# Gated linear attention beside an expert layer: the second half of a sequence attends the first by scores instead of a state

## The chip, the cores and the metric

One core of a Trainium2 chip runs the whole program in one launch. The metric is the device time in microseconds (us). The kernel before took 987.14 us in the median of three timed runs (986.79 to 999.11). The engines are PE (matmul), DVE (vector), ACT (scalar, which also applies the activation tables), POOL (GpSimd, which here also writes the scattered rows) and SP (which issues plain DMAs).

## The reference, cut to what matters

Two layers over 16 sequences of 256 tokens and width 128; each layer is x = x + s * silu(ffn(xn)), where xn is the normed x and s an attention of xn. The change is in the first attention, a gated linear attention with 4 heads (keys of 128, values of 32):

```
q = (x @ Wq).reshape(B, T, H, DK)
k = (x @ Wk).reshape(B, T, H, DK)
v = (x @ Wv).reshape(B, T, H, DV)
gk = jax.nn.log_sigmoid(x @ Wgk1 @ Wgk2 + bgk2) / GATE_NORM
...
G = jnp.cumsum(gc, axis=-2)
qg = qc * jnp.exp(G) * scale
k_intra = kc * jnp.exp(-G)
kg = kc * jnp.exp(G[..., -1:, :] - G)
A = jnp.where(jnp.tril(jnp.ones((C, C), bool)), A, 0.0)   # A = qg @ k_intra^T
o = A @ v + qg @ S
S = S * g_last + kg^T @ v
...
o = o * rsqrt(mean(o * o) + EPS) * gnw * silu(x @ Wg)
s = o.reshape(B, T, H * DV) @ Wo
```

The first layer's ffn is a top-2 mixture of 8 experts: each token's row is scattered to a list of its expert, the lists are worked through in groups of 512 rows, and the results scattered back. The second layer (softmax attention and 16 experts) is not touched.

## The kernel before

Each engine has its own program, written out in the order of one function, `walk` (L302), which calls the same step names on all engines. Semaphores (`sig`) link the engines, and a step's position in `walk` and in the step function is its place in the engine's queue.

**The attention of one batch b** (a sequence, `NB` = 16) takes five ticks. At tick t the function `gla(t, part)`, with parts 0, 1 and 2, works on several batches at once. The sequence is cut in two chunks of 128 tokens, u = 0 and 1:

- tick t = b: `gate_out` (PE, L478) and `gate_logs` (ACT, L980: two Abs, one Exp, one Ln), `gate_sigmoids` (DVE, L1498).
- tick b+1: `decays` on DVE (L1508) is the running sum over the tokens, one scan of 128x1040; `decays` on ACT (L996) makes its two exponentials, P and N; `chunk_ends` on POOL (L1911) multiplies four columns of P and N to the decay over the chunk; `queries_keys` (PE, L491) gives four banks, which `scaled` (DVE, L1537) multiplies by P and N.
- tick b+2: `keys_turned` (PE, L512) turns the first chunk's keys, `keys_moved` (ACT, L1015) copies them out; `scores` (PE, L520) multiplies keys and queries inside each chunk, as a 64x128 and a 64x64 block for each head and chunk; `masked` (DVE, L1520) applies the causal mask.
- tick b+3: `key_values` (PE, L532) makes the state of the first chunk, `states` (DVE, L1529) scales it, `outputs` (PE, L542) adds masked scores times values and, for the second chunk, queries times state.
- tick b+4: normalisation (`output_means` PE, `outputs_scale` ACT, `output_gates` POOL, `gated` DVE), `project` (PE, L561) and `attended` (ACT, L1043).

**Where the ticks lie.** Ticks 0 to 6 stand in the scatter stage, in which POOL writes the rows of all tokens to the expert lists. Ticks 7 to 19 stand in the experts loop, g = 0 to 18, where `TICKS` says which tick a round has: (7, 8, 9, 0, 10, 11, 0, 12, 13, 0, 14, 15, 0, 16, 0, 17, 18, 19, 0). A 0 is a round without a tick, called a bare round below. From tick 7 on (`OUTPUTS_EARLY`) some steps stand in another part. A round is, on every engine:

```
turn(0, g + 1)      # PE turns 512 rows of x, ACT: high part, DVE: low part
gla(t, 0)
ffn0(g, 0); ffn0(g, 1)  # PE up products in two halves, ACT tanh, DVE hidden
gla(t, 1)
ffn0(g, 2)          # PE down products of g - 1, DVE bias, POOL stores
gla(t, 2)
```

**Banks.** All products but the outputs and the gate product share a ring of four PSUM banks (`bank`, L393). A product takes the next bank and waits until the reader of its former contents is done. An up half (`expert_up`, L643) takes two banks. So the order in which steps take banks decides for whom PE waits: in a bare round the takes are turn, two for the first half, two for the second half, down, and the last bank of the second half is the one of the turn, freed by DVE's low part (L1589).

**Names in the rows.** L616 turning of x rows, L559 means, L488 gate product, L539 state product, L661 to L663 up products, L675 down products, L517 key turning; on ACT L990 first gate logs, L1093 tanh, L1019 copy of turned keys, L1005 and L1006 decay exponentials, L881 a table load; on DVE L1550 and L1552 scaled queries and keys, L1514 the scan, L1589 the low part, L1608 the bias; on POOL L1877 scatter of rows, L1896 store of y rows, L1916 `chunk_ends`.

## Time and profile before

| | before |
|---|---|
| timed runs, median (lowest, highest) | 987.14 us (986.79, 999.11) |
| the profiled execution's own time | 995.33 us |
| its span, first to last instruction | 993.3 us |
| mean granted TensorE clock | 0.856 of full |
| PE busy | 738.5 us, 74% |
| DVE busy | 646.1 us, 65% |
| ACT busy | 616.1 us, 62% |
| POOL busy | 453.9 us, 46% |

Busy time is a mean over stages that have different limits. The stages are: norm and routing to 44 us, scatter with ticks 0 to 6 to 160.5, experts with ticks 7 to 19 to 380, and the second layer. The chain that ended last is put down to PE for 33%, ACT 19%, DVE 17%, issue 16% and POOL 9% of the span. The granted clock has two levels, 1.00 (2.4 GHz) and 0.50 (1.2 GHz); a value between them is a mean over a stretch in which it changed.

### The profile page before, as it was taken

The page shows a single profiled execution, that of the slowest core. Times are in us where ns is not written, and L with a number is a line of the kernel's source. Part 1 is how long each engine was busy: PE and PEld are TensorE (multiplying, and loading weights), DVE is VectorE, ACT ScalarE, POOL GpSimd, SP SyncE. Part 2 cuts the span into 40 slices and gives each one's busy share as a digit, 9 for nine tenths or more (in the row PEclk, how much of TensorE's full clock was granted, in tenths as well). Part 3 has the DMA queues.
Part 4 walks back from the last instruction along what each step waited for, and adds up shares of the span by engine and source line. Part 5 has one row for each costly group of instructions (what it writes and reads, how often), then busy time and mean ns, then how long its engine had stood idle before and what let it go on. Part 6 is the DMA issues. An engine that isn't in the chain of part 4 may idle for free.

```text
span 993.3 us, 21325 instructions
## 1 busy us (share of the span) xinstructions
PE 738.5 (74%) x8182; PEld 573.3 (58%) x8182; DVE 646.1 (65%) x1190; ACT 616.1 (62%) x1139; POOL 453.9 (46%) x484
## 2 busy tenths in 40 slices
PE   6756776989898992466954788687978888888650
PEld 4535555878887892344642445456756766766540
DVE  5765655766666643777567554575677777687647
ACT  5653455766667462675641434475778878878775
POOL 4485763242443454100004665223566666756632
PEclk8777879999999996678885777698999999999985
DMA  9811222011111113400003321300111111110054
GB/s 310 304 45 47 62 64 58 20 50 31 47 47 39 46 42 108 115 1 2 1 1 119 121 85 60 86 13 23 30 39 41 34 39 39 42 36 26 19 158 118
DMA packets 62357, 63.81 MB, mean 64 GB/s; under 512 B 7378, under 2 KB 52322, under 8 KB 62132
## 3 DMA queue, kind: packets, MB, share of 16 engines
q1 hardware_dynamic: 53300, 44.02, 15.1%
q0 software_dynamic: 8960, 18.43, 5.7%
q8 instruction: 68, 1.11, 0.5%
q14 instruction: 29, 0.24, 0.1%
HBM read 31.88 MB, written 30.55 MB: 63 GB/s over the span
## 4 chain that ended last, share of the span: by engine, by line
PE 33%; ACT 19%; DVE 17%; issue 16%; POOL 9%; DMA 2%; another core or an unknown queue 2%; SPq 0%; ACTq 0%; POOLq 0%; DVEq 0%
POOL xs L1877 6%; ACT arena L1220 4%; PE bank L721 4%; ACT L881 3%; PE bank L786 3%; PE bank L675 3%; PE bank L798 2%; PE bank L528 2%; POOL ys L1896 2%; DVE arena L1644 2%; DVE arena L1737 2%; ACT arena L1121 2%; DVE arena L1624 1%; DVE arena L1642 1%
## 5 line engine op out<-in xcount | busy, mean ns | idle before, releaser
L1896 POOL DMA_INDIRECT ys<-arena x152 | 172.3, 1134 | 178.4 <-ACT arena L1149 56.3
L1877 POOL DMA_INDIRECT xs<-arena x128 | 131.3, 1026 | 77.1 <-issue 33.5
L1220 ACT ACTIVATE arena<-bank 128x512 f32<-128x512 f32 x192 | 99.1, 600 | 83.6 <-PE bank L786 62.1
L1737 DVE TENSOR_REDUCE arena<-bank 128x2 bf16<-128x512 f32 (+1 forms) x192 | 119.0, 682 | 41.9 <-PE bank L759 37.8
L661 PE MATMUL bank<-arena 128*128 128x128 bf16 x608 | 105.9, 220 | 6.4 <-DVE arena L1589 3.3
L662 PE MATMUL bank<-arena 128*128 128x128 bf16 x608 | 105.9, 220 | 0.0
L663 PE MATMUL bank<-arena 128*128 128x128 bf16 x608 | 105.9, 220 | 0.0
L881 ACT ACT_TABLE_LOAD x72 | 92.4, 1283 | 1.3
L1725 DVE SCALAR_TENSOR_TENSOR arena<-arena,bank 128x512 bf16<-128x512 bf16 x64 | 46.0, 746 | 71.2 <-ACT arena L1193 68.0
L721 PE MATMUL bank<-arena 128*128 128x256 f32 x256 | 67.2, 410 | 0.9 <-issue 0.9
L661 PEld LDWEIGHTS bank<-arena 128*128 x608 | 60.2, 99 | 9.6 <-issue 6.5
L662 PEld LDWEIGHTS bank<-arena 128*128 x608 | 59.8, 98 | 0.3
L663 PEld LDWEIGHTS bank<-arena 128*128 x608 | 59.6, 98 | 0.0
L1828 POOL TENSOR_TENSOR arena<-arena 128x4 f32<-128x4 f32 x16 | 16.2, 1010 | 87.9 <-DVE arena L1323 80.7
L721 PEld LDWEIGHTS bank<-arena 128*128 128x128 f32 x256 | 50.7, 208 | 9.3 <-issue 2.6
L691 PE MATMUL bank<-arena 128*128 x320 | 44.1, 296 | 14.5 <-POOL arena L1942 11.7
L1942 POOL TENSOR_TENSOR arena<-arena 128x1024 f32<-128x1024 f32 x19 | 44.7, 2355 | 20.4 <-ACT arena L1130 19.0
L691 PEld LDWEIGHTS bank<-arena 128*128 128x128 f32 x320 | 42.1, 211 | 17.5 <-issue 17.0
L756 PE MATMUL bank<-arena 32*128 32x256 bf16 (+1 forms) x512 | 22.8, 273 | 38.5 <-DVE arena L1725 14.9
L501 PE MATMUL bank<-arena 128*128 128x256 bf16 x128 | 37.9, 296 | 11.8 <-DVE arena L1518 7.5
L1193 ACT ACTIVATE arena<-bank 128x512 bf16<-128x512 f32 x64 | 36.6, 609 | 16.1 <-PE bank L721 15.6
L1937 POOL TENSOR_TENSOR arena<-arena 128x512 f32<-128x512 f32 x40 | 40.6, 1035 | 10.7 <-DVE arena L1644 10.7
(236 smaller groups left out, 2063.9 us busy)
## 6 DMA issues: line engine op xcount, KB each, us to landing
xs<-arena SPq DMA_DIRECT2D x19, 516.0 KB, 7.2
arena<-xs SPq DMA_DIRECT2D x38, 258.0 KB
arena<-ys SPq DMA_DIRECT2D x32, 256.0 KB, 5.1
arena<-in_MF SPq DMA_DIRECT2D x8, 512.0 KB
ys<-arena POOLq DMA_INDIRECT x152
arena<-in_x SPq DMA_DIRECT2D x8, 256.0 KB, 5.7
arena<-in_W SPq DMA_DIRECT2D x8, 256.0 KB
xs<-arena POOLq DMA_INDIRECT x128
```

Source lines behind the costliest of these rows:

```text
L661: mm(o, hi, b[:, 0, c4], stop=False)
L662: mm(o, hi, b[:, 1, c4], start=False, stop=False)
L663: i = mm(o, lo, b[:, 0, c4], start=False)
L691: i = mm(k[:, 128 * j:128 * j + 128], tb[g % 2][:, h0:h0 + 128], D, start=(c == 0), stop=(c == 1))
L721: j = mm(k[:, 256 * z:256 * z + 256], Wqk[:, c:c + 128], xnT[:, 256 * b:256 * b + 256])
L881: eng.preload_act_table_set(name)
L1220: act(PT[kt_][:, i, gs[0]:gs[0] + len(gs), :], bank_of["s2", b, n, i][:, :].rearrange("p (g q) -> p g q", q=w), ACT.Exp, scale=8 ** -0.5). ...
L1725: stt(T, hiT[n % 2], low_of[n // 2], bank_of["qk1", b, n][:, :], ALU.mult, ALU.add).then_inc(m_qk_moved.sem, 1)
L1737: red(negM[b % 2][:, u, 32 * i + gs[0]:32 * i + gs[0] + len(gs)], kv_, op=ALU.max, negate=True).then_inc(m_max.sem, 1)
L1877: eng.indirect_dma_start(xs[l][:, :], bass.IndirectOffsetOnAxis(ap=slot_i[l][:, m:m + 1], axis=0), xrow[:, t, :], None).then_inc(rows_move ...
L1896: eng.indirect_dma_start(ys[l][:, :], bass.IndirectOffsetOnAxis(ap=yid[g % 4][:, j:j + 1], axis=0), y[:, 128 * j:128 * j + 128], None).the ...
L1942: tt(T, T, U, ALU.mult).then_inc(f1_h.sem, 1)
```

## The change

The state is gone. The second chunk attends the first by scores as well: DVE's `keys_shifted` multiplies the first chunk's scaled keys by the decay over the chunk, PE's `scores` makes four more blocks of 128x128 (`cross`) of them and the second chunk's queries, ACT's `crossed` copies the blocks from PSUM, and `outputs` multiplies the values of the first chunk with them. `keys_turned`, `keys_moved`, `key_values`, `states` and POOL's `chunk_ends` go. The blocks inside a chunk are made whole, one of 128x128 for each head and chunk.

From tick 7 on the places change: `scores`, `crossed` and `masked` stand in part 0, ahead of the up products, the gate logs and the gating; the scan (`decays` on DVE) stands at the end of part 2 of the tick before. POOL's store of the second pair of y rows waits for `o_mean` instead of `kv`.

```diff
...
-        bufK, bufKT = [sb(1024) for _ in range(2)], [sb(512) for _ in range(2)]
+        bufK, bufKX, bufX = [sb(1024) for _ in range(2)], [sb(512) for _ in range(2)], [sb(512) for _ in range(2)]
...
-        bufS = [sb(128) for _ in range(2)]
-        ends = [sb(4) for _ in range(4)]
+        ends = [sb(4) for _ in range(2)]
...
-            def keys_turned(b):
-                k4 = bufK[b % 2].rearrange("p (h c) -> p h c", h=4)
-                k = bank(("kt", b), kt_moved.at(b))
-                eng.wait_ge(*qk_mul.at(b))
-                for h in range(4):
-                    i = eng.transpose(k[:, 128 * h:128 * h + 128], k4[:, h, 0:128], ident)
-                i.then_inc(kt.sem, 1)
...
                 for u in range(2):
                     k, n = bank(("att", b, u), att_masked.at(b, u)), slice(128 * u, 128 * u + 128)
-                    early, late = slice(128 * u, 128 * u + 64), slice(128 * u + 64, 128 * u + 128)
+                    if u == 0:
+                        eng.wait_ge(*qk_mul.at(b))
                     for h in range(4):
-                        mm(k[0:64, 128 * h:128 * h + 128], k4[:, h, early], q4[:, h, n])
-                        i = mm(k[64:128, 128 * h + 64:128 * h + 128], k4[:, h, late], q4[:, h, late])
+                        i = mm(k[:, 128 * h:128 * h + 128], k4[:, h, n], q4[:, h, n])
                     i.then_inc(att.sem, 1)
-            def key_values(b):
-                KT, v = bufKT[b % 2], bufV[b % 3]
-                k = bank(("kv", b), state.at(b))
-                eng.wait_ge(*kt_moved.at(b))
-                eng.wait_ge(*v_moved.at(b))
+                k = bank(("cross", b), cross_moved.at(b))
+                eng.wait_ge(*k_shifted.at(b))
                 for h in range(4):
-                    i = mm(k[:, 32 * h:32 * h + 32], KT[:, 128 * h:128 * h + 128], v[:, 32 * h:32 * h + 32])
-                i.then_inc(kv.sem, 1)
+                    i = mm(k[:, 128 * h:128 * h + 128], bufKX[b % 2][:, 128 * h:128 * h + 128], q4[:, h, 128:256])
+                i.then_inc(cross.sem, 1)
...
-                v, S, A4, o = bufV[b % 3], bufS[b % 2], bufAT[b % 2], o_banks[b % 2]
-                q4 = bufQ[b % 3].rearrange("p (h c) -> p h c", h=4)
+                v, A4, o = bufV[b % 3], bufAT[b % 2], o_banks[b % 2]
                 if b > 1:
                     eng.wait_ge(*o_y.at(b - 2))
+                eng.wait_ge(*v_moved.at(b))
                 for u in range(2):
                     eng.wait_ge(*att_masked.at(b, u))
                     for h in range(4):
                         mm(o[32 * h:32 * h + 32, 128 * u:128 * u + 128], v[:, 128 * u + 32 * h:128 * u + 32 * h + 32], A4[:, u, h, :], start=(u == 0), stop=(u == 0))
-                eng.wait_ge(*state.at(b))
+                eng.wait_ge(*cross_moved.at(b))
                 for h in range(4):
-                    i = mm(o[32 * h:32 * h + 32, 128:256], S[:, 32 * h:32 * h + 32], q4[:, h, 128:256], start=False)
+                    i = mm(o[32 * h:32 * h + 32, 128:256], v[:, 32 * h:32 * h + 32], bufX[b % 2][:, 128 * h:128 * h + 128], start=False)
                 i.then_inc(o_mm.sem, 1)
...
                     if at(t):
                         gate_out(t)
-                    if at(t - 3):
-                        key_values(t - 3)
+                    if at(t - 2) and t >= OUTPUTS_EARLY:
+                        scores(t - 2)
                 elif part == 1:
                     if at(t - 3) and t >= OUTPUTS_EARLY:
                         outputs(t - 3)
-                    if at(t - 2):
-                        keys_turned(t - 2)
+                    if at(t - 2) and t < OUTPUTS_EARLY:
                         scores(t - 2)
                     if at(t + 1):
...
-            def keys_moved(b):
-                eng.wait_ge(*kt.at(b))
+            def crossed(b):
+                eng.wait_ge(*cross.at(b))
                 if b >= 2:
-                    eng.wait_ge(*kv.at(b - 2))
-                act(bufKT[b % 2], bank_of["kt", b][:, :], ACT.Copy).then_inc(kt_moved.sem, 1)
+                    eng.wait_ge(*o_mm.at(b - 2))
+                act(bufX[b % 2], bank_of["cross", b][:, :], ACT.Copy).then_inc(cross_moved.sem, 1)
...
                     if at(t - 4):
                         outputs_scale(t - 4)
+                    if at(t - 2) and t >= OUTPUTS_EARLY:
+                        crossed(t - 2)
                     if at(t):
                         gate_logs(t)
                 elif part == 1:
-                    if at(t - 2):
-                        keys_moved(t - 2)
+                    if at(t - 2) and t < OUTPUTS_EARLY:
+                        crossed(t - 2)
                     if at(t - 1):
...
-            def states(b):
-                kv_, S = (a.rearrange("p (h d) -> p h d", h=4) for a in (bank_of["kv", b][:, 0:128], bufS[b % 2]))
-                eng.wait_ge(*kv.at(b))
-                eng.wait_ge(*p_ends.at(b))
-                if b > 1:
-                    eng.wait_ge(*o_mm.at(b - 2))
-                tt(S, kv_, bc(ends[b % 4], 2, [128, 4, 32]), ALU.mult).then_inc(state.sem, 1)
+            def keys_shifted(b):
+                k4, kx = (a.rearrange("p (h c) -> p h c", h=4) for a in (bufK[b % 2], bufKX[b % 2]))
+                P, N = (a.rearrange("p (h u s) -> p h u s", h=4, u=2) for a in (bufP, bufN))
+                tt(ends[b % 2], P[:, :, 0, 128], N[:, :, 1, 64], ALU.mult).then_inc(k_shifted.sem, 1)
+                eng.wait_ge(*k_shifted.at(b, 0))
+                eng.wait_ge(*qk_mul.at(b))
+                if b >= 2:
+                    eng.wait_ge(*cross.at(b - 2))
+                tt(kx, k4[:, :, 0:128], bc(ends[b % 2], 2, [128, 4, 128]), ALU.mult).then_inc(k_shifted.sem, 1)
             def scaled(b):
...
-                    if at(t - 3):
-                        states(t - 3)
+                    if at(t - 2) and t >= OUTPUTS_EARLY:
+                        masked(t - 2)
                     if at(t - 4) and t >= OUTPUTS_EARLY:
                         gated(t - 4)
-                    if at(t - 1) and t >= OUTPUTS_EARLY:
-                        decays(t - 1)
                 elif part == 1:
-                    if at(t - 2):
+                    if at(t - 2) and t < OUTPUTS_EARLY:
                         masked(t - 2)
                     if at(t + 1):
                         gate_low(t + 1)
...
-                elif at(t - 1):
-                    scaled(t - 1)
+                else:
+                    if at(t - 1):
+                        scaled(t - 1)
+                        keys_shifted(t - 1)
+                    if at(t) and t + 1 >= OUTPUTS_EARLY:
+                        decays(t)
...
-                    eng.wait_ge(*(kv.at(t - 3) if 0 < t < 19 else up[0].at(g, 1) if g < 18 else down[0].at(17)))
+                    eng.wait_ge(*(o_mean.at(t - 4) if t else up[0].at(g, 1) if g < 18 else down[0].at(17)))
...
-            def chunk_ends(b):
-                P, N = (a.rearrange("p (h u s) -> p h u s", h=4, u=2) for a in (bufP, bufN))
-                eng.wait_ge(*pn.at(b))
-                if b >= 4:
-                    eng.wait_ge(*state.at(b - 4))
-                tt(ends[b % 4], P[:, :, 0, 128], N[:, :, 1, 64], ALU.mult).then_inc(p_ends.sem, 1)
...
-                if part == 1 and 0 <= t - 1 < NB:
-                    chunk_ends(t - 1)
...
```

**PE, from the turning to the first up product of an attention round.** Before, where `qk_scaled`, `s0_done` and the like are semaphores named after the step that sets them:

```order
L616 MATMUL bank<-arena 128x128 [waits ld_rows0,qk_scaled]
L616 MATMUL bank<-arena 128x128 x3
L627 TENSOR_LOAD arena
L559 MATMUL bank<-arena 128x256 [waits o_squared]
L488 MATMUL bank<-arena 128x256 [waits decay,gate1_lo]
L488 MATMUL bank<-arena 128x256
L488 MATMUL bank<-arena 128x256 [waits decay]
L488 MATMUL bank<-arena 128x256
L539 MATMUL bank<-arena 128x32 [waits v_moved,k_turned_moved,qk_scaled]
L539 MATMUL bank<-arena 128x32 x3
L661 MATMUL bank<-arena 128x128 [waits x_lo0,s0_done,qk_scaled]
```

Of the change, the same place (L600 is the turning, L544 the means, L486 the gate product, L519 the scores, L524 the cross blocks, L645 the first up product):

```order
L600 MATMUL bank<-arena 128x128 [waits ld_rows0,qk_scaled]
L600 MATMUL bank<-arena 128x128 x3
...
L544 MATMUL bank<-arena 128x256 [waits o_squared]
L486 MATMUL bank<-arena 128x256 [waits decay,gate1_lo]
...
L519 MATMUL bank<-arena 128x128 [waits qk_scaled]
L519 MATMUL bank<-arena 128x128 x3
L519 MATMUL bank<-arena 128x128 [waits qk_scaled]
L519 MATMUL bank<-arena 128x128 x3
L524 MATMUL bank<-arena 128x128 [waits k_shifted,s0_done]
L524 MATMUL bank<-arena 128x128 x3
L645 MATMUL bank<-arena 128x128 [waits x_lo0,att_masked]
```

The scores stand ahead of the ups, and the ups wait for the mask's and the low part's banks.

**ACT, from the high part to the tanh of an attention round** behind a bare one. Before:

```order
L1082 ACTIVATE arena<-bank 128x512 [waits up0,turned0]
L881 ACT_TABLE_LOAD
L1039 ACTIVATE arena<-bank,arena 128x256 [waits o_gated,o_mean]
L1041 ACTIVATE arena<-arena 128x256 [waits o_rs]
L990 ACTIVATE arena<-bank 128x4x128 [waits exp_decay,gate2]
...
L881 ACT_TABLE_LOAD
L1093 ACTIVATE arena<-bank 128x512 [waits f0_h,up0] x2
L1019 ACTIVATE arena<-bank 128x512 [waits kv,k_turned]
L1005 ACTIVATE arena<-arena 128x1040 [waits chunk_ends,qk_scaled,decay]
```

Of the change (L1068 high part, L1003 `crossed`, L974 first gate logs, L1079 tanh, L989 first decay exponential):

```order
L1068 ACTIVATE arena<-bank 128x512 [waits up0,turned0]
L865 ACT_TABLE_LOAD
L1023 ACTIVATE arena<-bank,arena 128x256 [waits o_gated,o_mean]
L1025 ACTIVATE arena<-arena 128x256 [waits o_rs]
L1003 ACTIVATE arena<-bank 128x512 [waits o_mm,att_cross]
L974 ACTIVATE arena<-bank 128x4x128 [waits exp_decay,gate2]
...
L865 ACT_TABLE_LOAD
L1079 ACTIVATE arena<-bank 128x512 [waits f0_h,up0] x2
L989 ACTIVATE arena<-arena 128x1040 [waits k_shifted,qk_scaled,decay]
```

The copy moved from behind the tanh to ahead of the gate logs.

**DVE, from the scaled keys of one round to the hidden values of the next.** Before:

```order
L1552 TENSOR_TENSOR arena<-bank,arena 128x512 [waits att,qk]
L1552 TENSOR_TENSOR arena<-bank,arena 128x512 [waits qk]
L1589 SCALAR_TENSOR_TENSOR arena<-bank,arena 128x512 [waits x_hi0]
L1535 TENSOR_TENSOR arena<-bank,arena 128x128 [waits o_mm,chunk_ends,kv]
L1558 TENSOR_TENSOR arena<-bank,arena 128x256 [waits wo_mm,o_gate]
L1514 SCALAR_TENSOR_TENSOR arena<-arena 128x1040 [waits decay]
```

Of the change (L1541 scaled keys, L1519 and L1524 `keys_shifted`, L1500 the scan, L1580 the low part, L1513 `masked`, L1547 `gated`):

```order
L1541 TENSOR_TENSOR arena<-bank,arena 128x512 [waits att,qk]
L1541 TENSOR_TENSOR arena<-bank,arena 128x512 [waits qk]
L1519 TENSOR_TENSOR arena<-arena 128x4
L1524 TENSOR_TENSOR arena<-arena 128x512 [waits att_cross,qk_scaled,k_shifted]
L1500 SCALAR_TENSOR_TENSOR arena<-arena 128x1040 [waits decay]
L1580 SCALAR_TENSOR_TENSOR arena<-bank,arena 128x512 [waits x_hi0]
L1513 COPY_PREDICATED arena<-arena,bank 128x512 [waits o_mm,att]
L1513 COPY_PREDICATED arena<-arena,bank 128x512 [waits att]
L1547 TENSOR_TENSOR arena<-bank,arena 128x256 [waits wo_mm,o_gate]
```

The scan moved ahead of the low part, and two mask steps stand between the low part and the gating.

## Rows read from the trace of the kernel before

**Rows 1.** Busy time by stretch: PE, PEld, DVE, ACT, POOL, clock, DMA share, GB/s

```profile
160.50:380.00 219.50, 197.48 (x2430) 180.78 (x2430) 139.07 (x223) 146.74 (x225) 87.34 (x107) 0.96 0.15 41
```

**Rows 2.** Who PE waited for, 160 to 345 us: total, times, longest

```profile
PE bank L517 <- ACT arena L1093: 16.7, 9, 2.8
```

**Rows 3.** Timeline of PE: start, duration, engine, line, operation, count

```profile
177.35 0.60 PE L616 MATMUL bank<-arena 128*128 128x128 f32 x4
...
192.93 0.60 PE L616 MATMUL bank<-arena 128*128 128x128 f32 x4
...
194.24 0.98 PE L539 MATMUL bank<-arena 128*128 128x32 f32 x8
...
208.51 0.60 PE L616 MATMUL bank<-arena 128*128 128x128 f32 x4
209.24 0.22 PE L661 MATMUL bank<-arena 128*128 128x128 bf16 x1
...
211.98 2.00 PE L675 MATMUL bank<-arena 128*128 128x128 f32 x16
213.82 0.60 PE L616 MATMUL bank<-arena 128*128 128x128 f32 x4
...
332.71 0.60 PE L616 MATMUL bank<-arena 128*128 128x128 f32 x4
```

**Rows 4.** Timeline of ACT in the round of t=9

```profile
194.89 1.06 ACT L990 ACTIVATE arena<-bank 128x512 f32<-128x512 f32 x2
...
199.44 1.09 ACT L1093 ACTIVATE arena<-bank 128x512 f32<-128x512 f32 x2
200.79 0.60 ACT L1019 ACTIVATE arena<-bank 128x512 f32<-128x512 f32 x1 [0.26 <-PE bank L517]
201.28 1.06 ACT L1005 ACTIVATE arena<-arena 128x1040 f32<-128x1040 f32 x1
```

**Rows 5.** Timeline of DVE, end of round t=9, and the scan of t=10

```profile
206.66 1.28 DVE L1550 SCALAR_TENSOR_TENSOR arena<-bank,arena 128x512 f32<-128x512 f32 x2
207.86 1.28 DVE L1552 TENSOR_TENSOR arena<-bank,arena 128x512 f32<-128x512 f32 x2
209.78 0.69 DVE L1589 SCALAR_TENSOR_TENSOR arena<-bank,arena 128x512 bf16<-128x512 f32 x1 [0.64 <-issue]
...
218.48 2.32 DVE L1514 TENSOR_TENSOR_SCAN arena<-arena 128x1040 f32<-128x1040 bf16 x1
```

**Rows 6.** Timeline of ACT in the round of t=10

```profile
221.76 1.09 ACT L1093 ACTIVATE arena<-bank 128x512 f32<-128x512 f32 x2
```

**Rows 7.** Groups by form: count, busy us, mean ns, idle before

```profile
L1702 DVE TENSOR_TENSOR arena<-arena 128x512 f32<-128x512 f32 x8 | 5.5, 692 | 0.3
```

**Rows 8.** Waits of POOL, 50 to 160 us; timeline of PE at 160 us

```profile
POOL arena L1916 <- ACT arena L1006: 12.2, 4, 5.2
...
160.57 0.66 PE L616 MATMUL bank<-arena 128*128 128x128 f32 x2 [4.46 <-DMA arena<-xs]
```

**Rows 9.** Busy time by stretch around idle stretches of PE, columns as in rows 1

```profile
222.40:224.50 2.10, 2.09 (x16) 1.76 (x18) 1.27 (x2) 1.38 (x3) 0.00 (x0) 0.50 0.55 126
...
200.10:202.70 2.60, 2.53 (x36) 2.13 (x36) 2.00 (x3) 2.34 (x4) 0.00 (x0) 1.00 0.46 102
563.30:565.40 2.10, 0.00 (x0) 0.00 (x0) 0.70 (x2) 0.00 (x0) 1.49 (x3) 1.00 0.73 146
565.40:565.90 0.50, 0.44 (x2) 0.20 (x2) 0.50 (x1) 0.00 (x0) 0.50 (x1) 1.00 0.99 386
...
591.50:593.60 2.10, 0.00 (x0) 0.00 (x0) 0.71 (x2) 0.00 (x0) 1.51 (x4) 1.00 0.73 144
593.60:594.30 0.70, 0.67 (x2) 0.29 (x2) 0.70 (x2) 0.00 (x0) 0.70 (x1) 0.50 0.94 381
```

**Rows 10.** Timeline of POOL in the round of t=9

```profile
197.25 1.99 POOL L1896 DMA_INDIRECT ys<-arena  x1 [0.30 <-issue]
```

More of the change, by code:

```diff
@@ L246, in build @@
         gate2, gate2_ln, decay = sig("gate2", 2), sig("gate2_ln", 4), sig("decay", 5)
-        pn, p_ends = sig("exp_decay", 2), sig("chunk_ends")
+        pn, k_shifted = sig("exp_decay", 2), sig("k_shifted", 2)
         xq_hi, xq_lo = sig("chunk_hi"), sig("chunk_lo")
@@ L250, in build @@
         vv, v_moved = sig("v"), sig("v_moved")
-        kt, kt_moved = sig("k_turned"), sig("k_turned_moved")
+        cross, cross_moved = sig("att_cross"), sig("att_cross_moved")
         att, att_masked = sig("att", 2), sig("att_masked", 2)
-        kv, state = sig("kv"), sig("state")
         o_mm, o_sq, o_mean, o_rs, o_gate, o_y = sig("o_mm"), sig("o_squared"), sig("o_mean"), sig("o_rs", 2), sig("o_gate"), sig("o_gated")
@@ L1001, in decays @@
                     eng.wait_ge(*qk_mul.at(b - 1))
-                    eng.wait_ge(*p_ends.at(b - 1))
+                    eng.wait_ge(*k_shifted.at(b - 1, 0))
                 else:
```

## The prediction, made before the change was run

> **What bounds the kernel now.** I read the page's slices first, then the busy time by stage, then whom PE waits for in the stage in which the change lives, then the timelines of one round there, engine by engine. In the experts-and-attention stage (160.5 to 380 us) PE is busy for 197.5 of 219.5 us, DVE for 139 and ACT for 147 [rows 1]: none is full on its own, so a round is as long as its chain of waits. PE's main wait there is the one before the key turning (L517), for ACT's tanh (L1093): 9 times, 16.7 us, the longest 2.8 [rows 2].
>
> I count a round from the start of the turning of its x rows on PE (L616, time T) to the next. The round of t=9 runs from 192.93 to 208.51, 15.58 us, and the bare round behind it to 213.82, 5.31 us. From 177.35 to 332.71, 155.36 us, lie eight attention rounds, t=8 to 15, and four bare ones of about 5.3 (21.3), so the eight take 134.1 [rows 3].
>
> An attention round has two segments. **T to tanh**: turning, means and gate product keep PE until T+1.31 (194.24) [rows 3]; ACT starts the gate logs at T+1.96 (194.89) and the tanh pair at T+6.51 (199.44) [rows 4]. **Tanh to the next T**, 9.07 us: ACT copies the turned keys behind the tanh pair (200.79) and starts the decay exponentials at tanh+1.84 (201.28) [rows 4]; the gate product's copy, the chunk's low part and the gate sums follow, then DVE writes the scaled queries (206.66 to 207.94) and keys (207.86 to 209.14) [rows 5]. The next turning needs the bank of the second query product, free at 207.94; PE, busy since the end of its wait, comes there at 208.51.
>
> **The change, part by part.** *PE work.* An f32 product 128x128x128 is two passes; the 16 passes of L675 from 211.98 to the turning at 213.82 make 0.115 us a pass [rows 3]. Per batch 4 turnings, 16 half-block products in pairs and 4 state products go; 8 whole blocks and 4 cross blocks come, 24 passes, 2.76 us. By the counts PE loses some 0.5 us a batch, which alone shortens no round in which PE waits.
>
> *ACT: `crossed` stands ahead of the gate logs.* Its copy waits for the last cross block. PE can begin the scores at T+1.31 and needs 2.76, so the block is there at about T+4.1. The copy holds ACT for 0.49 (200.79 to 201.28) [rows 4]; the logs start at T+4.6 instead of T+1.96, the tanh at T+9.2 instead of T+6.51: +2.7. *ACT: `keys_moved` is gone from behind the tanh.* The exponentials start at tanh+1.13 instead of +1.84, and all down to the scaled queries moves up by 0.71: the bank is free at tanh+7.8 and the next T is at tanh+7.85 instead of +9.07, PE no longer being the later one, since its scores are done: -1.2. Together a round is 9.2+7.85 = 17.05 us. Behind a bare round (t=10, 12, 14) ACT also loads a table first, and its tanh is at T+7.94 now (221.76 from 213.82) [rows 3, 6]; that load ends before the cross block does, so these rounds become 17.05 as well. Eight rounds: 136.4 against 134.1, **+2.3**; so little because the three reload rounds, the longest now, get shorter and the five others longer.
>
> *DVE: the scan stands ahead of the x low part.* The keys are scaled by 209.14, tanh+9.70, and 0.71 sooner is tanh+8.99 = T+1.14. Then come `keys_shifted`, a 128x4 product (0.2, an estimate: nearest is the 128x512 one, of which it is a small part) and a 128x512 product from SBUF (0.69) [rows 7], and the scan (2.32), all before L1589 (0.69), whose end frees the turn bank [rows 5]: about T+4.95, against T+1.96 now (210.47). In a bare round the ring of four banks gives that bank to the second half of the up products. Both halves take 2.74 now (209.24 to 211.98) and the down products 1.84 [rows 3], so the next T is at 4.97+1.37+1.84 = 8.2 against 5.3. A scan stands in front of four bare rounds: 4 x 2.9 = **+11.5**. In attention rounds the ups wait for that bank too, and for `masked` (T+5.7), but they end by T+8.5, before ACT is ready for the tanh at T+9.2: nothing; that ACT wait is the cover, and without it each would cost up to 2.
>
> *Round t=7* starts its logs as late, +2.7, and gains the 0.7: **+2.0**. *Rounds t=16 to 19* have no logs, so the 0.5 us of PE work shows in each, and t=16 stalls less: **-3**, an estimate with bounds 0 and -5.
>
> *Scatter stage, t=1 to 6.* `chunk_ends` goes from POOL, where scatter descriptors stand behind it; it held them for 12.2 us in four waits on ACT's exponentials. Behind the last scatter PE waits 4.46 us for the rows, until 160.57 [rows 8]: at most that is to be had. Against it, `crossed` stands ahead of the exponentials there, where PE runs at half clock in part, and I count some 3 us of new ACT wait over t=3 and t=6. **-1**, bounds -4 and +4.
>
> *POOL's store* waits for `o_mean` instead of `kv`, which comes sooner in a round: nothing, stores wait for no one else here.
>
> *Clock.* In a bare round PE would be idle from about T+2.55 to T+4.95, 2.4 us. After an idle of 2.1 the clock was still 1.00 once (565.4) and 0.50 once (593.6), after 2.8 it was 0.50 (222.4), after 1.4 it was 1.00 (200.1) [rows 9]. If it falls, 5.5 us of work behind the idle do what 2.75 would: 4 x 2.75 = 11. The rows split, so I take half, **+5.5**. [...]
>
> Sum: 2.3+11.5+2.0-3-1+5.5 = **+17.3**. The profiled execution took 995.3 (span 993.3); the median of the timed runs is 987.1, 8.2 below it and inside their spread (986.8 to 999.1). The sum is a difference of rounds and is set on the median: **1004.5 us**.
>
> **The rivals.** *More clock lost (0.14).* In t=10, 12 and 14 PE has its outputs done at T+7.8 and the tanh at T+9.8: 2.0 idle, between the 1.4 that held and the 2.1 that went both ways. If it falls there, three rounds pay 1.5 to 3 each and all bare rounds pay: 987+12+11+4.5 to 9 = 1015 to 1019. Against: the 2.8 stalls of just these rounds, with their low clock, go.
>
> *The scan stays off the path (0.13).* If the second ups of a bare round had their bank as early as now, 11.5 and 5.5 would fall away: 988, no change. For it: DVE is busy only 63% of the stage [rows 1]. Against: the low part is behind the scan in program order, and the ring has no other bank.
>
> *POOL late (0.06).* The scan now lies where POOL writes the first two y rows of a round. A y row written beside the scan took 1.99 us [rows 10]. The Trainium skill (GPSIMD Engine Reference, Specifications) says that DVE and GpSimd contend for SBUF when DVE reads two SBUF inputs; the 1.99 agrees. Were two rows late by 1 us in eight rounds and waited for, 1004.5 would become 1012 to 1020. Against: no wait of DVE for y stores shows before the stage's end.
>
> *It gets faster (0.05).* One mechanism: the cross block is there when ACT arrives. Then `crossed` costs 0.5, the tanh is at T+7.0 and a round 14.9, eight 119, -15; with the -3 and -4 of the last rounds and the scatter stage and the scan hidden, 967. It turns on the block's end: at T+2.0 it would hold, at T+4.1 it doesn't, and PE cannot begin before T+1.31 [rows 3].
>
> **How the numbers follow.** The forecast (0.62) has its own range, 994 (clock held, scatter stage -4) to 1013 (clock lost in all bare rounds, scatter stage +2). The range of 8 in 10, 991 to 1018, leaves out the fast case (0.05), most of the no-change case (0.08) and the far ends of the slow rivals (0.07). Under 2% (19.7 us, 1006.9) a measurement of this kernel can hardly tell a change from none. Of the forecast 0.22 lies above that, with 0.14 and 0.06 of the two slow rivals: slower 0.42; faster 0.04; within 2% 0.54.
>
> **What would show it.** In the profile after: gate logs 4.6 us behind T (1.96 now), ACT waiting for the cross block ahead of its copy; attention rounds of 17.0, all alike; bare rounds of 8 us, PE waiting 2.4 us for the low part; no tanh wait before scores; PE at 0.50 or at 1.00 behind the bare rounds' idle, which settles the clock term; less than 4.46 us of waiting for rows at the stage's start. I am wrong if attention rounds stay at 15.6 or less, if bare rounds stay at 5.3, or if the scatter stage moves by over 4 us.

## The result and the profile after

The changed kernel takes 1000.85 us in the median of 18 runs (992.10 to 1004.39), the kernel before, beside it, 988.46 (984.21 to 999.11). The ratio is 1.0119, with a 95% interval of 1.0099 to 1.0140: about 12 us slower, inside the 2% that was named as no change. The profiled execution took 999.84 us, its span is 998.0, and the mean granted clock 0.867 (0.856 before).

The page's busy times of the changed kernel, over the whole span:

```profile
PE 729.2 (73%) x7862; PEld 565.5 (57%) x7862; DVE 650.7 (65%) x1206; ACT 612.6 (61%) x1139; POOL 457.1 (46%) x468
```

PE has 9 us less to do and the kernel takes longer: busy time decides nothing here, as [rows 1] said. Whom the engines wait for, 150 to 345 us, in the changed kernel (total, times, longest; L645 is the first up product, L473 stands behind the outputs, L499 is the query and key product, L1079 the tanh, L1003 the copy of the cross blocks, L524 their product):

```profile
PE bank L645 <- DVE arena L1580: 13.1, 8, 2.2
PE bank L473 <- ACT arena L1079: 12.3, 8, 2.3
PE bank L499 <- DVE arena L1504: 4.9, 7, 2.2
PE bank L600 <- DMA arena<-xs: 2.1, 2, 1.6
...
ACT arena L1079 <- PE bank L647: 19.1, 8, 4.2
ACT arena L1003 <- PE bank L524: 16.2, 9, 3.4
```

The one wait of [rows 2], 16.7 us for the tanh ahead of the key turning, has become three: for DVE's low part (L1580) ahead of the ups, for the tanh (L473), and for the chunk's low part (L499). ACT has a new one, 16.2 us in nine rounds, for the cross blocks.

The round of t=9 of the changed kernel, which begins at 189.27 and answers to [rows 3 to 6] (timeline; L600 turning, L974 first gate logs, L989 first exponential, L1541 scaled keys, L1524 `keys_shifted`, L1500 the scan, L1580 low part), and the bare round behind it:

```profile
189.27 0.66 PE L600 MATMUL bank<-arena 128*128 128x128 f32 x4
...
192.43 1.06 PE L524 MATMUL bank<-arena 128*128 128x128 f32 x8
...
193.52 0.60 ACT L1003 ACTIVATE arena<-bank 128x512 f32<-128x512 f32 x1 [2.14 <-PE bank L524]
...
194.01 1.08 ACT L974 ACTIVATE arena<-bank 128x512 f32<-128x512 f32 x2
...
194.76 0.22 PE L645 MATMUL bank<-arena 128*128 128x128 bf16 x1 [1.28 <-DVE arena L1580]
...
198.59 1.09 ACT L1079 ACTIVATE arena<-bank 128x512 f32<-128x512 f32 x2
...
199.24 0.67 PE L473 MATMUL bank<-arena 128*80 128x128 f32 x4 [0.84 <-ACT arena L1079]
...
199.56 1.07 ACT L989 ACTIVATE arena<-arena 128x1040 f32<-128x1040 f32 x1
...
204.72 1.28 DVE L1539 SCALAR_TENSOR_TENSOR arena<-bank,arena 128x512 f32<-128x512 f32 x2
...
206.06 0.65 PE L600 MATMUL bank<-arena 128*128 128x128 f32 x4
...
207.30 0.69 DVE L1524 TENSOR_TENSOR arena<-arena 128x512 f32<-128x512 f32 x1
...
207.91 2.32 DVE L1500 TENSOR_TENSOR_SCAN arena<-arena 128x1040 f32<-128x1040 bf16 x1
...
210.15 0.67 DVE L1580 SCALAR_TENSOR_TENSOR arena<-bank,arena 128x512 bf16<-128x512 f32 x1
...
210.96 0.22 PE L645 MATMUL bank<-arena 128*128 128x128 bf16 x1 [2.16 <-DVE arena L1580]
...
214.14 0.60 PE L600 MATMUL bank<-arena 128*128 128x128 f32 x4
```

The round takes 16.79 us (15.58 before): the copy at T+4.25 has waited 2.14 for the cross blocks, the logs are at T+4.74, the tanh at T+9.32, the next turning at tanh+7.47. The bare round takes 8.08 (5.31 before): DVE has `keys_shifted` and the scan in front of the low part, and PE stands for 2.16 us.

All rounds from the first turning on, each the distance between two turnings in the timeline of PE (us). In t=7 the first turning is that of the very first rows. In brackets, where a bare round follows:

| round | before | before, run again | changed |
|---|---|---|---|
| first turning at | 160.6 | 154.9 | 150.4 |
| t=7 | 16.8 | 16.8 | 22.2 |
| t=8, 9 (bare) | 15.6, 15.6 (5.3) | 15.6, 15.6 (5.3) | 16.7, 16.8 (8.1) |
| t=10, 11 (bare) | 19.7, 15.6 (5.3) | 19.7, 15.6 (5.3) | 16.7, 16.8 (8.1) |
| t=12, 13 (bare) | 18.3, 15.6 (5.3) | 18.3, 15.6 (5.3) | 16.7, 16.8 (9.7) |
| t=14, 15 (bare) | 18.6, 15.2 (5.4) | 18.6, 15.2 (5.4) | 17.4, 15.6 (9.0) |
| t=16 (bare), t=17 | 14.9 (5.3) 10.5 | 14.9 (5.3) 10.4 | 13.0 (5.3) 10.0 |
| first joining step of the layers | 393.0 | 387.5 | 398.8 |
| from there to the end of the span | 600.3 | 602.9 | 599.2 |

The part behind the joining step isn't touched by the change; it takes 597.4 to 603.5 us in this kernel, the one before and the eight runs up to e8, so the differences in that row are spread. The changed kernel loses between first turning and join (248.4 us against 232.7) and has 4.5 to 10 us of it back from the scatter stage.

### The profile page after: what moved, and what is told of

Its sections match the earlier page's. It is cut to its first block, busy times and chain, and to the rows that moved or that the text cites. A ratio compares the mean times of both kernels' runs of the same rounds, so it can differ in the third digit from the quotient of the medians.

```text
span 998.0 us, 20675 instructions
## 1 busy us (share of the span) xinstructions
PE 729.2 (73%) x7862; PEld 565.5 (57%) x7862; DVE 650.7 (65%) x1206; ACT 612.6 (61%) x1139; POOL 457.1 (46%) x468
## 4 chain that ended last, share of the span: by engine, by line
PE 25%; ACT 16%; DVE 15%; issue 9%; another core or an unknown queue 3%; POOL 1%; DMA 1%; SPq 0%; ACTq 0%; DVEq 0%
ACT arena L1206 5%; PE bank L705 3%; PE bank L782 3%; PE bank L770 3%; ACT L865 2%; PE bank L675 2%; PE bank L659 2%; DVE arena L1728 2%; DVE arena L1635 2%; ACT arena L1107 1%; PE bank L784 1%; DVE arena L1615 1%; DVE arena L1633 1%; DVE arena L1716 1%
## 5 line engine op out<-in xcount | busy, mean ns | idle before, releaser
L1887 POOL DMA_INDIRECT ys<-arena x152 | 167.3, 1101 | 225.7 <-DVE arena L1599 98.3
L645 PE MATMUL bank<-arena 128*128 128x128 bf16 x608 | 106.6, 221 | 21.5 <-DVE arena L1580 16.7
L645 PEld LDWEIGHTS bank<-arena 128*128 x608 | 59.3, 98 | 25.8 <-issue 15.1
L1589 DVE SCALAR_TENSOR_TENSOR arena<-arena,bank 128x512 f32<-128x512 f32 x36 | 23.8, 686 | 56.8 <-ACT arena L1079 55.2
L1819 POOL TENSOR_TENSOR arena<-arena 128x4 f32<-128x4 f32 x16 | 16.2, 1010 | 88.9 <-DVE arena L1309 81.9
L675 PE MATMUL bank<-arena 128*128 x320 | 43.7, 294 | 14.5 <-POOL arena L1924 11.8
L675 PEld LDWEIGHTS bank<-arena 128*128 128x128 f32 x320 | 41.6, 209 | 17.6 <-issue 17.0
L499 PE MATMUL bank<-arena 128*128 128x256 bf16 x128 | 38.2, 299 | 16.8 <-DVE arena L1504 10.8
L740 PE MATMUL bank<-arena 32*128 32x256 bf16 (+1 forms) x512 | 22.2, 268 | 36.2 <-DVE arena L1716 14.7
L782 PE MATMUL bank<-arena 128*32 128x256 f32 x512 | 44.4, 398 | 3.6 <-issue 2.0
```

The lines of the kernel that those rows point to most:

```text
L645: mm(o, hi, b[:, 0, c4], stop=False)
L675: i = mm(k[:, 128 * j:128 * j + 128], tb[g % 2][:, h0:h0 + 128], D, start=(c == 0), stop=(c == 1))
L782: mm(k[32 * i:32 * i + 32, 256 * m:256 * m + 256], V[:, 0, 4 * g + i, :], PT[0][:, i, g, :], start=(m == 0), stop=False)
L1887: eng.indirect_dma_start(ys[l][:, :], bass.IndirectOffsetOnAxis(ap=yid[g % 4][:, j:j + 1], axis=0), y[:, 128 * j:128 * j + 128], None).the ...
```

## The experiments

The first eight of the twelve ran on one chip, where the kernel before took 987 to 991. The last four ran on another, on which both kernels are some 40 us faster; 28 of these lie behind the join (571 to 574 us there in every kernel). These four are read by their ratios and by the rounds. Below, "eight" is the sum of the rounds t=8 to 15 and "bare" the sum of the four bare rounds between t=9 and t=16: 134.0 and 21.3 in the kernel before (134.2 and 21.4 when run again), 133.5 and 34.9 in the changed one.

**b2: the kernel before once more.**

> The kernel before, unchanged, for a second trace of it: the one shown took 995.3 us where the median of its runs is 988.5. The theory (the change took 10 us out of the scatter stage) expects the first turning of x rows at 160 us again, give or take 2. The rival (the trace shown was a slow one in just that stage, and the change gains only some 3 us there) expects it at 153 to 155.

Its one run took 992.42. Its rounds repeat within 0.1 us, its first turning does not: 154.9 against 160.6. POOL's waits for the exponentials, 12.2 us in [rows 8] (12.0 of them between 45 and 150 us), are 5.7 in this execution (waits of POOL, 45 to 150 us):

```profile
POOL arena L1916 <- ACT arena L1006: 5.7, 3, 5.0
```

So the trace on which the prediction was made was a bad case of the scatter stage, and the stage moves by over 5 us between two executions of one kernel.

**e2: the scan back behind the gating.**

```diff
-                    if at(t) and t + 1 >= OUTPUTS_EARLY:
-                        decays(t)
+                    if at(t - 1) and t >= OUTPUTS_EARLY:
+                        decays(t - 1)
```

> The changed kernel with the DVE scan back in its old place (part 0, behind the gating) and nothing else moved. Theory (the scan ahead of the low part costs only the bare rounds, the attention rounds are set by ACT's copy): bare rounds of 5.3 us instead of 8.1, 8.1, 9.7 and 9.0, attention rounds unchanged at 16.7, so 13 to 14 us less than the changed kernel, about 987. Rival (the scan ahead of the low part also sets the attention rounds, whose up products wait for the low part): those get shorter too, by 1 us or more each, and the time is 979 or less.

Measured: 990.44 (ratio 1.0028, 0.9987 to 1.0068); bare 21.7, eight 138.6. The bare rounds are back at 5.3 to 5.9: the scan ahead of the low part is what made them long. But only 13.2 us are gained there and 5.1 lost in the attention rounds, which the expectation had as unchanged. PE now stands once, for 2.28 us, where the changed kernel stands for 1.28 and 0.84 (in t=11 and 13 for 1.28 and some 0.7); the row in the timeline of PE, then the clock by stretch (columns as in [rows 1]; the clock is the third number from the end):

```profile
239.86 0.50 PE L473 MATMUL bank<-arena 128*80 128x128 f32 x1 [2.28 <-ACT arena L1079]
```

```profile
237.00:240.00 3.00, 0.72 (x25) 0.46 (x14) 0.16 (x1) 2.97 (x4) 0.49 (x2) 0.98 0.44 115
240.00:243.00 3.00, 3.00 (x15) 3.00 (x16) 1.59 (x4) 3.00 (x7) 0.00 (x0) 0.50 0.00 1
```

The rounds t=10 to 15 come to 17.2 to 17.7, with the clock at 0.50 behind the idle; t=8 and 9, with the same 2.28 us of idle, take 16.7 and 16.8. In the rounds behind a bare one the changed kernel stands there for 1.98 to 2.03 us itself, nearly as long as e2. The scan's place thus had a second effect: in the plain rounds it cut PE's idle in two.

**e3: the copy of the cross blocks behind the logs, the scan left where the change put it.**

```diff
-                    if at(t - 2) and t >= OUTPUTS_EARLY:
-                        crossed(t - 2)
                     if at(t):
                         gate_logs(t)
+                    if at(t - 2) and t >= OUTPUTS_EARLY:
+                        crossed(t - 2)
```

> The changed kernel with ACT's copy of the cross blocks behind the gate logs instead of ahead of them. Theory (ACT's wait for the cross block sets the attention rounds): logs at T+2.0, tanh at T+7.0, the second tanh at T+8.3 since the up products end then, rounds of about 15.2 instead of 16.75, bare rounds unchanged; 12 us less, about 989. Rival (PE and DVE set them, the ACT wait is only in parallel): rounds stay within 0.4 of 16.75 and the time at 998 to 1001.

Measured: 986.59 (0.9984, 0.9938 to 1.0029); eight 123.3, bare 36.5 (9.70, 9.71, 9.71, 7.39). ACT's wait for the cross blocks is gone and the rounds are 14.5 to 15.9, in all 10.2 us less than in the changed kernel. Round t=7 takes 16.4 instead of 22.2.

**e4: both moves.** The edits of e2 and e3 together.

> The changed kernel with both moves: scan back in part 0 and ACT's copy behind the gate logs. Theory: attention rounds of 14.5 us, bare rounds of 5.3, together 31 us less than the changed kernel, about 969, which is also under the kernel before. Rival (the costs overlap, one hides the other): the time is no lower than the better of the two single moves, some 985.

Measured: 971.46 (0.9822, 0.9775 to 0.9869); eight 119.2, bare 22.9. ACT in the round of t=9, which begins at 183.83 and ends at 198.36 (timeline; L1068 high part, L865 table load):

```profile
183.83 0.33 PE L600 MATMUL bank<-arena 128*128 128x128 f32 x1
...
185.84 1.07 ACT L974 ACTIVATE arena<-bank 128x512 f32<-128x512 f32 x2
186.94 1.06 ACT L976 ACTIVATE arena<-arena 128x1024 f32<-128x1024 f32 x1
188.03 1.06 ACT L978 ACTIVATE arena<-arena 128x1024 f32<-128x1024 f32 x1
189.00 0.58 ACT L1003 ACTIVATE arena<-bank 128x512 f32<-128x512 f32 x1
189.60 1.28 ACT L865 ACT_TABLE_LOAD   x1
190.89 1.09 ACT L1079 ACTIVATE arena<-bank 128x512 f32<-128x512 f32 x2
...
198.36 0.65 PE L600 MATMUL bank<-arena 128*128 128x128 f32 x4
```

The logs start at T+2.0, as in [rows 4]; the copy behind them finds its block done and waits for nothing; the tanh is at T+7.1, the next turning 7.47 behind it. PE's wait for the tanh is gone; what is left, 160 to 345 us, is 13.5 us in waits of at most 2.1:

```profile
PE bank L645 <- ACT arena L1003: 7.0, 8, 1.8
PE bank L499 <- DVE arena L1504: 4.7, 8, 2.1
PE bank L645 <- DVE arena L1541: 1.8, 3, 0.6
```

This version beats both kernels: 1.8% less than the one before by the ratio, 16 us between the medians measured together. Against the changed kernel the single moves gave 10.4 and 14.3 us and both together 29.4, so neither hides the other.

**e5: the algebra alone,** every step where it stood before: scores and copy in part 1 behind the ups and the tanh, mask there too, scan behind the gating.

> The change's algebra alone (no state, cross blocks, whole score blocks), with every step where it stood before: scores, copy of the cross blocks and mask behind the logs, scan behind the gating. Theory (a round is its chain of waits, not its work): the tanh comes at T+6.5 as before, but the scores and the copy of the cross blocks stand between the tanh and the exponentials, so the exponentials wait for the cross block: attention rounds of about 17.2 us (16.7 to 17.6), bare rounds 5.3, PE's new wait inside the rounds for the exponentials' products; time about 992 (988 to 997). Rival (the 0.5 us of PE work a batch saved counts by itself): rounds of 15.1, time about 983 to 985.

Measured: 1004.23 (1.0121, 1.0066 to 1.0176); eight 147.9, bare 22.9. Four of the five plain rounds are 17.1 to 17.2, as expected (t=15 takes 16.8), but t=10, 12 and 14 take 20.1, 21.1 and 21.1. The round of t=10 (timeline of PE and ACT, then the clock by stretch; L519 the scores, L1075 the tanh, L1001 the copy, L987 the first exponential):

```profile
222.99 1.27 PE L519 MATMUL bank<-arena 128*128 128x128 f32 x9 [3.44 <-ACT arena L1075]
...
227.50 0.60 ACT L1001 ACTIVATE arena<-bank 128x512 f32<-128x512 f32 x1 [4.08 <-PE bank L524]
227.99 1.06 ACT L987 ACTIVATE arena<-arena 128x1040 f32<-128x1040 f32 x1
```

```profile
220.00:222.90 2.90, 0.00 (x0) 0.00 (x0) 1.56 (x1) 2.87 (x4) 2.23 (x3) 1.00 0.07 23
222.90:227.00 4.10, 4.01 (x23) 4.01 (x24) 2.68 (x4) 0.52 (x2) 0.00 (x0) 0.65 0.32 80
```

PE stands 3.44 us for the tanh, makes scores and cross blocks largely at the low clock, and the exponentials wait for the copy. I had left this out of the expectation, and it is 10 of the 12 us by which that was too low. Less work on PE earned nothing; without the move of the scores ahead of the ups the new algebra costs as much as the whole change does.

**e6: the kernel before, with `chunk_ends` on DVE** behind the scaled keys instead of on POOL.

> The kernel before with one edit: the product of four columns (chunk_ends) goes from POOL to DVE, behind the scaled keys. Theory (my scatter term): POOL no longer waits for the exponentials there (5 to 12 us of waits in the scatter stage), so the scatter is done earlier: the experts stage starts 1 to 4 us sooner and the time is 1 to 4 us less than before, 983 to 986, rounds unchanged at 15.6 and 5.3. Rival: the scatter is bound elsewhere and the start of the experts stage stays within 0.5 us: time 987.

Measured: 985.63 against 991.41 (0.9943, 0.9906 to 0.9980). POOL's wait for the exponentials is not in its list of waits any more; the first turning is at 156.4, between the two of the kernel before. Of the gain, 2.7 us in this trace are a clock that held in t=10 (17.0 instead of 19.7 us), which the edit doesn't explain. A gain for the edit, then, but its size is read from neither the trace nor the interval.

**e7: the changed kernel, with the product of four columns on POOL,** in its old place.

> The changed kernel with one edit: the product of four columns goes back from DVE to POOL's queue, where it stood before the change. Theory (scatter term): POOL waits for the exponentials in the scatter stage again, which starts the experts stage 1 to 4 us later: 1002 to 1005. Rival (those waits are covered): no change, 1000 to 1001, the POOL waits there with no shift of the stage's end.

Measured: 1010.85 (1.0181, 1.0119 to 1.0243), by the ratios 6 us more than the changed kernel, where 1 to 4 were expected; the two intervals overlap. The waits are back (45 to 150 us):

```profile
POOL arena L1907 <- ACT arena L991: 8.9, 4, 3.8
```

The first turning is at 157.7. Over all traces of this chip: with that product on POOL (before, b2, e7) 160.6, 154.9 and 157.7, mean 157.7; the six kernels with the new algebra and without it 150.4 (changed), 153.8, 153.8, 152.4, 154.9 and 153.2, mean 153.1. That is 4.6 us, more than the 1 I took, but it is an estimate and not a measurement of the one product: either group spreads by 4.5 to 5.7 us, the second differs from the first in its algebra too, and e6, the old algebra with the product off POOL, is at 156.4, only 1.3 below the first mean.

**e8: the changed kernel with half blocks in the scores.**

```diff
-                        i = mm(k[:, 128 * h:128 * h + 128], k4[:, h, n], q4[:, h, n])
+                        mm(k[0:64, 128 * h:128 * h + 128], k4[:, h, early], q4[:, h, n])
+                        i = mm(k[64:128, 128 * h + 64:128 * h + 128], k4[:, h, late], q4[:, h, late])
```

> The changed kernel with the scores inside a chunk made as before the change, a block of 64x128 and one of 64x64 for each head and chunk instead of one of 128x128: 8 more products, issued in pairs, some of them smaller. Theory (equal work on PE, by pass counts): scores end within 0.3 us of where they do now, cross block and copy too, attention rounds 16.6 to 17.0 and the time within 2 us of the changed kernel, 999 to 1003. Rival (the whole blocks were the cheaper form): the copy and the logs come 0.5 us or more later in each of nine rounds, 1005 or more.

Measured: 1009.67 (1.0176, 1.0109 to 1.0243); eight 137.0, bare 38.0 (9.70, 9.72, 9.71, 8.90). A miss. The copy is at T+4.54 instead of T+4.25, less than the rival asked for. The eight rounds take 3.5 us more than in the changed kernel and the bare ones 3.1, and the larger part of this is the clock: it falls in all four bare rounds behind the same 2.16 us of idle as in the changed kernel, and in t=10, 12 and 14 behind 2.07 to 2.10 us of idle ahead of L473.

**e9 to e12: is it the clock?** If the bare rounds of 9.7 us are bare rounds of 8.1 with a fallen clock, work that PE does for nobody in the middle of the idle should shorten them. e9 is the changed kernel again; e10 (changed), e11 (e3) and e12 (e8) have in each bare round, ahead of the second half of the up products:

```diff
+                if l == 0 and j == 2 and 0 < g < 18 and not TICKS[g] and TICKS[g - 1] < 16:
+                    for _ in range(20):
+                        mm(o_banks[TICKS[g - 1] % 2][:, 0:128], up_weights(l, g, 1, 0)[0], b[:, 0, 0:128])
```

> The changed kernel once more, as the yardstick for the three filled kernels of the same job. Both theories expect a ratio to the kernel before of 1.012 (1.008 to 1.016), about 1001, bare rounds of 8.1 where the clock is held and 9.0 to 9.7 where it falls.

> The changed kernel with 20 more products in each of the four bare rounds (two bf16 operands that are there already, into a bank that nobody reads): they stand between the two halves of the up products, where PE waits about 2.1 us for the low part, and take about 1.1 us of that wait. Theory (the bare rounds of 9.0 to 9.7 are the low clock behind that idle): all four bare rounds take 8.1, though PE has more to do; against the changed kernel of the same job 1.5 to 3 us less, about 998. Rival (those rounds are long for another reason, or the products themselves delay the second half): bare rounds of 8.1 to 9.7 as before, or all longer by up to 1.1 us, 1000 to 1005.

> The kernel with the copy of the cross blocks behind the logs (e3_copy_behind_logs), whose bare rounds took 9.7, 9.7, 9.7 and 7.4, with the same 20 products in each bare round. Theory (clock): bare rounds of 8.1 or less, about 5 us less than without the products: 981 to 983. Rival: bare rounds stay at 9.7 and the time at 986 to 988.

> The changed kernel with half blocks in the scores (e8_half_blocks), whose bare rounds took 9.7, 9.7, 9.7 and 8.9, with the same 20 products in each bare round. Theory (clock): bare rounds of 8.1, about 5 us less than without the products, and of what half blocks cost only the attention rounds' share is left (17.0 instead of 16.75 us, some 2 us in all): 1002 to 1005. Rival (half blocks make the bare rounds long by themselves): 9.7 stays, 1007 to 1010.

| | time (before 947.21) | ratio and interval | bare rounds |
|---|---|---|---|
| e9 | 962.20 | 1.0165 (1.0128 to 1.0202) | 8.08, 9.76, 8.08, 7.39 |
| e10, filled | 960.16 | 1.0136 (1.0085 to 1.0186) | 8.08, 8.08, 8.08, 7.39 |
| e11, e3 filled | 944.53 | 0.9971 (0.9954 to 0.9988) | 8.09, 8.07, 8.08, 7.38 |
| e12, e8 filled | 964.07 | 1.0178 (1.0144 to 1.0213) | 8.08, 7.38, 8.08, 7.39 |

The first bare round of e3 (timeline of PE, then the clock by stretch):

```profile
205.30 0.22 PE L645 MATMUL bank<-arena 128*128 128x128 bf16 x1 [2.16 <-DVE arena L1580]
```

```profile
205.30:209.30 4.00, 4.00 (x35) 4.00 (x36) 1.14 (x2) 0.60 (x1) 1.20 (x3) 0.61 0.37 99
```

And of e11, the same two views:

```profile
195.10 0.22 PE L648 MATMUL bank<-arena 128*128 128x128 bf16 x1 [1.04 <-DVE arena L1583]
```

```profile
195.00:199.00 4.00, 3.90 (x46) 3.91 (x47) 1.76 (x3) 0.69 (x2) 1.28 (x3) 1.00 0.35 98
```

With 1.04 us of idle the clock held in all twelve filled bare rounds; without the products it fell in 11 of 20 (two in the changed kernel, three in e3, one in e7, four in e8, one in e9). In the bare rounds the 20 products cost nothing, and a round in which the clock holds is 1.6 us shorter, filled or not. Only e9 of the unfilled kernels ran on the chip of the filled ones, so the chip could be the reason; what speaks against it are the other idles. Of all PE idles of 0.8 to 1.5 us between 160 and 350 us none is followed by a lower clock in the next 3 us, 48 on the first chip and 34 on the second; of the 22 of 1.6 to 1.8 us 5 are, and of those of 1.9 to 2.3 us, 30 of 47 and 8 of 15. So the rival, rounds that are long for another reason, is out. In time it doesn't show: e10 is 2.0 us below e9, with overlapping intervals, e11's ratio is 0.0013 below e3's where 5 us were expected, and e12's isn't below e8's at all. e9 is also a warning: one and the same kernel loses the clock in the third and fourth bare round in one execution and in the second in another. In e12 the attention rounds grew to 17.0 to 18.0 (139.4 in all, 137.0 in e8), which took 2.4 of the 7.1 us that the bare rounds gave back; e12 stays 3.9 us above e10. Why half blocks lose the clock more often wasn't found out.

## Why the prediction was right, and where it wasn't

The forecast was 1004.5 with a range of 991 to 1018, and the time is 1000.9. The sum said +17.3; up to the join, scatter stage included, the changed trace is 11.3 us behind b2, and the timed difference is 12. (Over the whole span it is 7.6: the untouched part behind the join happened to be 3.7 shorter.) Term by term, against the rounds (b2, whose first turning is nearer to those of the later traces):

| term | predicted | measured |
|---|---|---|
| eight attention rounds | +2.3 | -0.7 |
| bare rounds, scan ahead of the low part | +11.5 | +10.3 |
| clock in the bare rounds | +5.5 | +3.2 |
| t=7 | +2.0 | +5.3 |
| t=16 to 19 | -3 | -2.3 |
| scatter stage | -1 | -4.5 |
| sum | +17.3 | +11.3 |

(The clock's share is what 9.71 and 9.01 exceed 8.08 and 7.39 by, the lengths of the third and fourth bare round where it holds, as in e10; the scan's is the rest, 3 x 8.08 + 7.39 - 21.4.) One sum of the prediction is off by itself: its low case, clock held and scatter stage at -4, gives 996 by its own terms and not 994; nothing hangs on it.

**Attention rounds.** The mechanism stands: the logs at T+4.74 (predicted 4.6), the tanh at T+9.32 (9.2), plain and reload rounds alike at 16.7 to 16.8 up to t=13. The mis-sized step is from the tanh to the next turning, 7.47 instead of 7.85: the exponentials start 0.97 behind the tanh, not 1.13, and the scaled queries 6.13 behind it (7.22 before), 1.09 sooner where I had moved them by 0.71. And I gave t=15, the shortest before, the same 17.05; it took 15.58, and t=14, in which the clock fell, 17.36. A gain of three long rounds against a loss of five short ones is a small difference, and 0.4 us a round decides its sign.

**The scan.** Its term was the largest and the best: bare rounds of 8.08 (8.2 predicted), PE standing 2.16 (2.4) for the low part. e2 shows the cause by undoing it, with the side effect on the clock that nobody's sum contained. My statement that the later low part costs nothing in attention rounds holds for their length: the ups wait 1.28 and end before ACT is ready.

**The clock.** Half of the four bare rounds was right as a count here, and that is luck: it was one of four in e9 and e7, three in e3, four in e8. The size was not: a fall costs 1.6 us in its round, not 2.75, since the clock is back before the round is over, as the stretch behind the third bare round's idle shows, with 0.57 as its mean:

```profile
295.00:299.00 4.00, 4.00 (x29) 4.00 (x27) 0.69 (x1) 0.60 (x1) 0.63 (x2) 0.57 0.37 87
```

A low clock does not follow each such idle: in the same trace the clock stays at 1.00 behind 2.16 us in the first bare round.

```profile
211.00:214.00 3.00, 3.00 (x39) 3.00 (x40) 1.09 (x2) 0.60 (x1) 1.15 (x2) 1.00 0.25 76
```

**t=7** failed as a step: I costed it as any other plain round. It opens the stage with rows that arrive in two pieces and with PE at a mean clock of 0.69 (150 to 155 us), so the cross blocks are late (the copy at T+7, not T+4.3), and PE then stands for 2.27 and 2.23 us and falls to the low clock again (L499, timeline of PE, then the clock by stretch; L473's wait ends at 163.08):

```profile
166.74 0.37 PE L499 MATMUL bank<-arena 128*128 128x256 bf16 x1 [2.23 <-DVE arena L1504]
```

```profile
168.00:172.00 4.00, 4.00 (x20) 2.87 (x19) 2.12 (x4) 0.00 (x0) 0.00 (x0) 0.50 0.00 0
```

e3 shows what this hangs on: with the copy behind the logs, and a clock no higher at the start (0.66 over its first 5 us), t=7 takes 16.4 us.

**The scatter stage** was mis-sized downwards and is the term with the least behind it: -4.5 against b2, -10.2 against the shown trace, beyond the 4 us that I had named as a bound and as one of the signs that I am wrong. The mechanism, POOL no longer waiting for the exponentials, is shown by e7's waits and supported by e6, the size only by means over a few traces that spread as widely. The wait for rows at the stage's start is 2.1 us (4.46 before), as the list of signs said. The errors of t=7 and of this term, 3.3 one way and 3.5 the other, cancel by luck; a part of the closeness of the sum is that.

**The rivals.** *More clock lost* asked for a clock that falls behind the tanh wait ahead of L473 in t=10, 12 and 14. It came true in one of the three: the clock held behind 1.98 and 2.02 us and fell in t=14 behind 2.03, where the round took 17.4 instead of 16.7 us (the clock by stretch, before and behind that wait):

```profile
303.00:307.00 4.00, 3.82 (x73) 3.37 (x71) 0.42 (x1) 3.79 (x6) 2.38 (x4) 1.00 0.13 42
...
309.00:312.00 3.00, 3.00 (x15) 2.98 (x15) 1.59 (x4) 3.00 (x7) 0.00 (x0) 0.50 0.00 0
```

At 0.6 us for that, and with two of four bare rounds, the time stayed below its 1015. *The scan stays off the path* fell with the bare rounds. *POOL late*: no wait of PE or DVE for its stores shows in the rounds. *It gets faster* asked for one thing, a cross block that is there when ACT arrives, and priced it at rounds of 14.9 and 967 with the scan hidden. The changed kernel does not have it; e4 does, with plain rounds of 14.5 and 971.5.

## What to carry over

An engine works its queue in order, so a copy of a product goes behind the work of its engine that doesn't need it, as far back as the product takes to be made: the logs here, and the same step costs 2.1 us of waiting or nothing. Before a long step (a scan of 2.3 us) is moved "where the engine is idle", look at the shortest round that it will stand in and at the buffer that the next step in that queue sets free. Count the chain from one round's start to the next and not the work removed: the algebra alone, with less work on PE, made the kernel 12 us slower, and two moves of a few lines turned the change from +12 us to some -17.

## What the runs showed of the hardware

The clock behind a PE idle of 2.0 to 2.3 us went both ways, in the same place of the same program and between two executions of it: behind 2.16 us it held in the first bare round and had fallen in the third (1.00 and 0.57 above), and in e9 it fell in the second. Behind 1.04 us it held in all twelve filled bare rounds, and behind all 82 idles of 0.8 to 1.5 us counted above. So one idle of 2.28 us (e2) cost more than two of 1.28 and 0.7 to 0.8 (t=11 and 13: 17.3 and 17.6 us against 16.8), and 1.1 us of useless products in the middle of an idle made bare rounds shorter by 1.6 us (9.70 to 8.09), which the total time didn't show.

The second thing is POOL beside DVE's scan. The same product, once with the scan beside it (191.13 to 193.45) and once with DVE idle, in the changed kernel (timeline of POOL; L1906 is the first of `output_gates`):

```profile
154.08 0.72 POOL L1906 TENSOR_TENSOR arena<-arena 128x256 f32<-128x256 f32 x1 [2.51 <-ACT arena L1025]
...
191.47 2.49 POOL L1906 TENSOR_TENSOR arena<-arena 128x256 f32<-128x256 f32 x1 [0.85 <-ACT arena L1025]
```

It takes 2.49 us instead of 0.72, and ends 0.5 us behind the scan. POOL's write of a y row shows the same, 1.80 to 1.92 us beside the scan and 0.95 to 1.05 otherwise. The Trainium skill (GPSIMD Engine Reference, Specifications) has the two engines contend for SBUF when DVE reads two SBUF inputs, and this trace agrees. In these rounds nobody waits for it: the gating has the low part and the mask in front of it.
